# Routing weights spread by DMA instead of by one-hot matmuls, in the second layer of a gated two-layer block

## The chip, the cores and the metric

The kernel runs on one core of one Trainium2 chip. The metric is the device time of one execution in microseconds (us). TensorE (PE in the profile) multiplies matrices, VectorE (DVE), ScalarE (ACT) and GpSimd (POOL) work on elements, SyncE (SP) issues the DMAs. Each engine runs its own instruction list in order, and the engines wait for one another on semaphores. SBUF is the on-chip memory, PSUM the banks that TensorE writes into.

## The reference, cut to what matters

```python
x = L0_attn_data                                     # (4, 512, 512), float32
x = x + s0(norm(x)) * silu(ffn0(norm(x)))            # first layer, untouched here
xn = layernorm(x)
s  = attention(xn)                                   # one head of 128, Wqkv, softmax, Wo
base_out   = xn @ base_w.T + base_b
res_hidden = xn @ A.T                                # 64 values of each row
probs      = softmax(xn @ router_w.T)                # 16 experts
topw, topi = top_k(probs, 2); topw = topw / (sum(topw) + 1e-6)
combine    = sum(one_hot(topi, 16) * topw[..., None], -2)
delta      = einsum('bse,bsr,eor->bso', combine, res_hidden, B)
x = x + s * silu(base_out + 0.5 * delta)
```

The last product, `delta`, is done as one matrix product over 16 x 64 = 1024 rows: row e*64+r is `combine[e] * res_hidden[r]`, and the weights `combine` must therefore be repeated 64 times each over the partitions.

## The kernel before, in words

There are four chunks (one for each of the 4 sequences of 512 rows), and two layers. The second layer takes them in turn, with a first chunk, a loop over two, and a last one. TensorE multiplies float32 numbers as pairs of a rounded part and a rest (`_hi`, `_lo`), three matmuls of 128x128 by 128x512 for a full product (`three`). ScalarE mostly makes the rounded parts, VectorE or GpSimd the rests.

In one chunk of the second layer TensorE does, in this order: `a` (the 64 hidden values and 16 logits), q, k, v; the transposes of the routing weights `comb`; `scores` of four tiles of 128 rows; `base` (the product with `base_w`, 12 matmuls a tile); the transposes of the probabilities (`probs_transpose`, kt 0 to 3); `lora` (the 1024-row product, 24 matmuls a tile); probabilities times v ("PV"); and `project` with Wo. Behind the third tile come the transposes of the next chunk's normalized rows.

Routing: VectorE finds the two largest weights in 19 short steps (`route`). The weights stand in `comb` twice, 32 columns apart. TensorE transposes them, ScalarE copies both copies to `combT`, VectorE replaces the second by the rest (L1129), and `spread` (L1322) multiplies `combT` by a matrix of zeros and ones, `pick`, so that a PSUM bank holds one expert's weight on each of 64 partitions. There are eight such products (kt 0 to 7) in a chunk, one matmul each, in two banks. VectorE's `prods` (L1068) multiplies the bank by `res` into one of three buffers of `prod`, ScalarE rounds it (`prod_hi`, L801), GpSimd makes the rest (`prod_lo`, L672), and `lora` uses both.

The order is written out by hand for each engine. `y`, which gathers `base` and `lora`, alternates between banks 2 and 3, so that the tiles 2 and 3 start `base` late in the chunk. The rows of the next chunk are loaded when the current ones have been transposed and the stores of the chunk before are done; VectorE takes their statistics (L369, L374) behind output tile 0 and 1 and normalizes them (L388), GpSimd makes the reciprocal root (L380, L382) behind its eight rests. GpSimd then multiplies gate and attention and adds the input (`gate`, L394 and L398).

Of the kernel before, what the change touches and what calls it, by code (L numbers as in the profile page):

```python
# [6 lines left out]
P = 128  # L7
BANK = 512

ALU = mybir.AluOpType  # L10
# [8 lines left out]
def block_mask_ffn_then_attention_lora_kernel(  # L19
# [27 lines left out]
    IT = w1.shape[0]  # L47
# [23 lines left out]
    mid_rows = mid.rearrange("b (t p) d -> b p t d", p=P)  # L71

    ctx = ExitStack()
    with ctx:
# [36 lines left out]
        comb = few.take("comb", [P, TT, 2 * Q])  # L111
# [27 lines left out]
        next_c = Span(span_c.start)  # L139
        pick_raw = raw_at("pick_raw", [P, KE, P], next_c.end)  # L140
        pick = next_c.take("pick", [P, KE, P], F32R)

        span_s = Span(phase(max(span_c.end, next_c.end)))
# [30 lines left out]
        prod_hi = next_1h.take("prod_hi", [P, KE, S], F32R)  # L174
        prod_lo = next_1l.take("prod_lo", [P, KE, S], F32R)
        res = next_1h.take("res", [P, S])
        combT = next_1l.take("combT", [P, S], F32R)
# [29 lines left out]
        prod = rest_t.take("prod", [P, 3, S])  # L207
# [88 lines left out]
        pick_ready = sem("pick_ready")  # L296
# [5 lines left out]
        comb_zero = sem("comb_zero")  # L302
        comb_hi = sem("comb_hi")
        comb_split = sem("comb_split")
# [18 lines left out]
        spread_done = sem("spread_done")  # L323
# [116 lines left out]
        y = [banks[2], banks[3]]  # L440
        sc = [banks[4], banks[5]]
        tr = [banks[6], banks[7]]
        NROUTE = 19
# [7 lines left out]
        def _(sp):  # L451
# [75 lines left out]
            def rows_out(c, place, to_next):  # L527

                for tt in range(TT):
                    if to_next:  # L530
                        turn(c + 1, 0, tt)
                    store_row(c, place, tt)
                sp.wait_ge(st_rows, c * TT * 16 + TT * 16)
                sp.sem_inc(g_free, 1)
# [5 lines left out]
            rows_out(0, mid_rows[0], True)  # L540
            with sp.Fori(1, CH - 1) as c:
                chunk(c, x_rows[c + 1], False)
                rows_out(c, mid_rows[c], True)
            chunk(CH - 1, mid_rows[0], True)
            rows_out(CH - 1, mid_rows[CH - 1], False)


            def chunk(c, source):
                g = c + CH
                sp.dma_start(x_res[:], mid_rows[c]).then_inc(ld_res, 16)  # L550
                if source is not None:
                    sp.wait_ge(xT_tr, g * TT + TT)
                    sp.dma_start(x_tile[:], source).then_inc(ld_x, 16)
                for tt in range(TT if source is not None else TT - 1):
                    sp.wait_ge(rows_done, g * TT + tt + 1)
                    sp.dma_start(out_rows[c][:, tt, :], g_tile[:, tt, :]).then_inc(st_out, 16)
                if source is not None:
                    sp.wait_ge(st_out, c * TT * 16 + TT * 16)
                    sp.sem_inc(g_free, 1)
                else:  # L560

                    for i in range(2):
                        sp.wait_ge(end_done, i + 1)
                        sp.dma_start(out_rows[c][:, TT - 1, half(i)], g_tile[:, TT - 1, half(i)]).then_inc(st_out, 16)
                    sp.wait_ge(st_out, CH * TT * 16 + 16)

            with sp.Fori(0, CH - 1) as c:
                chunk(c, mid_rows[c + 1])
            chunk(CH - 1, None)

        @block.gpsimd
        def _(gp):
# [39 lines left out]
            def next_layer():  # L612
# [7 lines left out]
                gp.wait_ge(t_done, CH)  # L620
                gp.memset(pick_raw[:], 0.0).then_inc(pick_ready, 1)
                for q in range(2):
                    gp.wait_ge(pick_ready, q + 1)
                    sq = pick_raw[:].rearrange("e k (h r) -> e k h r", r=R)
                    gp.affine_select(out=sq, in_=sq, compare_op=ALU.not_equal, fill=1.0, base=-q * Q,
                                     pattern=[[-EPT, KE], [-1, EPT], [0, R]], channel_multiplier=1).then_inc(pick_ready, 1)
                gp.wait_ge(pick_ready, 3)
                nc.gpsimd.tensor_copy(pick[:], pick_raw[:]).then_inc(pick_ready, 1)
# [39 lines left out]
            def chunk(c, last):  # L668

                for kt in range(KE):  # L670
                    gp.wait_ge(prod_hi_done, c * KE + kt + 1)
                    nc.gpsimd.tensor_tensor(prod_lo[:, kt, :], prod[:, kt % 3, :], prod_hi[:, kt, :].bitcast(F32),  # L672
                                            ALU.subtract).then_inc(prod_split, 1)
                if not last:
                    rows_rstd(gp, c + CH + 1)
# [8 lines left out]
        def _(act):  # L684
# [114 lines left out]
            def prods_hi(c, kt):  # L799
                act.wait_ge(prod_done, c * KE + kt + 1)  # L800
                nc.scalar.activation(prod_hi[:, kt, :], prod[:, kt % 3, :], ACT.Copy).then_inc(prod_hi_done, 1)  # L801
# [9 lines left out]
            def chunk(c, is_first, last):  # L811
# [8 lines left out]
                for j, src in enumerate((pj[1], sc[0], sc[1])):  # L820
                    if j == 2:
                        act.wait_ge(comb_tr, c + 1)
                        nc.scalar.activation(combT[0:2 * Q, :], tr[0][0:2 * Q, :], ACT.Copy).then_inc(comb_hi, 1)
# [8 lines left out]
                prods_hi(c, 0)  # L832
                prods_hi(c, 1)
                probs_exp(c, 1)
                prods_hi(c, 2)
                prods_hi(c, 3)
                probs_exp(c, 2)
                probs_exp(c, 3)
                prods_hi(c, 4)
                prods_hi(c, 5)  # L840
                probs_hi(c, 0)
                probs_hi(c, 1)
                probs_hi(c, 2)
                probs_hi(c, 3)
                prods_hi(c, 6)
                prods_hi(c, 7)
# [669 lines left out]
```

## Time and profile before

| | before |
|---|---|
| median of 3 runs | 650.63 us (649.14 to 651.12) |
| the profiled execution | 650.05 us, of which the span from the first to the last instruction is 648.2 us |
| TensorE busy | 632.3 us (98%) |
| VectorE, ScalarE, GpSimd busy | 446.3 (69%), 213.4 (33%), 240.0 us (37%) |
| granted TensorE clock | 0.999 of full |
| moved by DMA | 46.16 MB |

A busy share is an average over both layers. What an edit is worth is read where it stands: in the chain of waits, which follows the work that ended last back in time, and in the lists of instructions in order of time, which show what each engine waited for.

### The profile page before, as it was taken

To read this page: it belongs to the slowest core of one execution; us is meant where nothing else is said; L and a number is where in the kernel's file an instruction comes from. 1 tells how busy PE (TensorE), PEld (TensorE's weight loads), DVE (VectorE), ACT (ScalarE), POOL (GpSimd) and SP (SyncE) were. 2 spreads that over 40 slices of the span, in tenths; PEclk is the share of its full clock that TensorE was granted. 3 is DMA by queue.
4 is the path that set the end of the run, shared out by engine and by line. 5 is a ranking of instruction groups with operands and counts; after the bars stand their busy time and mean duration, and the time that the engine had idled before them with its cause. 6 is when DMAs were issued, how large, how long until landed. Compare 5 with 4: busy or idle time off the path is not lost.

```text
span 648.2 us, 8466 instructions
## 1 busy us (share of the span) xinstructions
PE 632.3 (98%) x2942; PEld 509.9 (79%) x2942; DVE 446.3 (69%) x716; ACT 213.4 (33%) x379; POOL 240.0 (37%) x188
## 2 busy tenths in 40 slices
PE   7999999999999999999999999999999999999997
PEld 3768787878888878888878787778878878887887
DVE  7987776787765777765777886655765857575633
ACT  3533333312223312223322243651255035314510
POOL 2355545650000740000742644582425433351441
PEclk9999999999999999999999999999999999999999
DMA  9940000022400022300153622050140013012000
GB/s 282 400 158 1 2 0 1 26 81 52 127 17 9 26 81 70 108 16 8 32 141 95 173 82 73 17 178 1 49 147 1 16 50 129 0 41 89 2 32 33
DMA packets 42575, 46.16 MB, mean 71 GB/s; under 512 B 25072, under 2 KB 25456, under 8 KB 41904
## 3 DMA queue, kind: packets, MB, share of 16 engines
q1 hardware_dynamic: 42544, 45.76, 22.1%
q8 instruction: 18, 0.29, 0.2%
q14 instruction: 13, 0.11, 0.1%
HBM read 31.85 MB, written 8.39 MB: 62 GB/s over the span
## 4 chain that ended last, share of the span: by engine, by line
PE 81%; DVE 12%; issue 3%; ACT 1%; POOL 1%; DMA 1%; DVEq 0%; POOLq 0%; ACTq 0%; SPq 0%
PE bank L418 73%; DVE counts L940 3%; PE bank L348 2%; DVE seg_top L926 2%; DVE eq L928 2%; PE bank L1205 1%; PE bank L1359 1%; DMA first<-counts 1%; PE bank L1183 1%; DVE h_lo L970 1%; PE bank L1322 1%; DVE h L961 1%; POOL g_tile L394 1%; PE bank L1224 1%; DVE ws_raw L994 0%
## 5 line engine op out<-in xcount | busy, mean ns | idle before, releaser
L418 PE MATMUL bank<-w_hi_t,h_hi 128*128 128x512 f32 x224 | 90.4, 404 | 0.7 <-DVE h_lo L970 0.4
L761 ACT ACTIVATE h_hi<-h 128x512 fp32r<-128x512 f32 x56 | 35.4, 633 | 162.9 <-DVE h L961 162.9
L418 PE MATMUL bank<-w_lo_t,h_hi 128*128 128x512 f32 x224 | 87.6, 391 | 0.0
L418 PE MATMUL bank<-xT_hi,w_hi_t 128*128 128x512 f32 x224 | 87.4, 390 | 0.1
L418 PE MATMUL bank<-w_hi_t,h_lo 128*128 128x512 f32 x224 | 87.4, 390 | 0.0
L418 PE MATMUL bank<-xT_hi,w_lo_t 128*128 128x512 f32 x224 | 87.2, 389 | 0.0
L418 PE MATMUL bank<-xT_lo,w_hi_t 128*128 128x512 f32 x224 | 87.1, 389 | 0.0
L940 DVE TENSOR_TENSOR_SCAN counts<-restart,eq 128x512 bf16<-128x512 bf16 (+1 forms) x56 | 76.0, 1357 | 2.4
L394 POOL TENSOR_TENSOR g_tile<-g_tile,s_tile 128x512 f32<-128x512 f32 x31 | 44.3, 1430 | 88.3 <-DVE g_tile L983 44.2
L926 DVE TENSOR_REDUCE seg_top<-bank 128x16 f32<-128x512 f32 (+1 forms) x64 | 39.5, 617 | 46.2 <-PE bank L1205 46.2
L672 POOL TENSOR_TENSOR prod_lo<-prod,prod_hi 128x512 fp32r<-128x512 f32 x32 | 40.6, 1291 | 57.9 <-ACT prod_hi L801 57.8
L970 DVE TENSOR_TENSOR h_lo<-h,h_hi 128x512 fp32r<-128x512 f32 x56 | 42.0, 751 | 27.0 <-ACT h_hi L761 25.4
L380 POOL TENSOR_TENSOR rstd<-mean_var,eps 128x4 f32<-128x4 f32 x8 | 1.6, 201 | 159.1 <-DVE mean_var L374 159.1
L740 ACT ACTIVATE h<-bank 128x512 f32<-128x512 f32 x56 | 33.5, 598 | 57.4 <-DVE h_lo L970 47.3
L418 PE MATMUL bank<-b_hi,prod_hi 128*128 128x512 f32 (+1 forms) x136 | 52.1, 383 | 0.0
L418 PE MATMUL bank<-b_hi,prod_lo 128*128 128x512 f32 (+1 forms) x136 | 51.3, 377 | 0.0
L418 PE MATMUL bank<-b_lo,prod_hi 128*128 128x512 f32 (+1 forms) x136 | 51.3, 377 | 0.0
L418 PEld LDWEIGHTS bank<-w_hi_t,h_hi 128*128 128x128 f32 x224 | 42.1, 188 | 10.7 <-DVE h_lo L970 2.3
L418 PEld LDWEIGHTS bank<-w_hi_t,h_lo 128*128 128x128 f32 x224 | 42.1, 188 | 9.4
L418 PEld LDWEIGHTS bank<-xT_hi,w_hi_t 128*128 128x128 f32 x224 | 42.0, 188 | 9.1 <-ACT s_tile L695 0.4
L418 PEld LDWEIGHTS bank<-xT_hi,w_lo_t 128*128 128x128 f32 x224 | 42.0, 188 | 8.7
L418 PEld LDWEIGHTS bank<-xT_lo,w_hi_t 128*128 128x128 f32 x224 | 42.1, 188 | 8.7
(191 smaller groups left out, 1300.5 us busy)
## 6 DMA issues: line engine op xcount, KB each, us to landing
w_raw<-in_w SPq DMA_DIRECT2D x28, 256.0 KB, 10.1
x_res<-in_x SPq DMA_DIRECT2D x4, 1024.0 KB, 8.5
mid_state<-g_tile SPq DMA_DIRECT2D x16, 256.0 KB, 2.1
x_tile<-mid_state SPq DMA_DIRECT2D x4, 1024.0 KB, 7.4
x_res<-mid_state SPq DMA_DIRECT2D x4, 1024.0 KB, 5.5
out<-g_tile SPq DMA_DIRECT2D x15, 256.0 KB, 2.0
x_tile<-in_x SPq DMA_DIRECT2D x3, 1024.0 KB, 5.6
b_raw<-in_lora_b SPq DMA_DIRECT2D x2, 1024.0 KB, 5.1
```

Of the source, the lines that this page charges most:

```text
L348: last = nc.tensor.transpose(rows_bank(g, tt)[:, k * P:(k + 1) * P], x_tile[:, tt, k * P:(k + 1) * P], ident[:])
L394: nc.gpsimd.tensor_tensor(g_tile[:, tt, :], g_tile[:, tt, :], s_tile[:, tt, :], ALU.mult).then_inc(s_free, 1)
L418: last = nc.tensor.matmul(dst, a, b, start=(start and n == 0), stop=(stop and n == len(mms) - 1))
L672: nc.gpsimd.tensor_tensor(prod_lo[:, kt, :], prod[:, kt % 3, :], prod_hi[:, kt, :].bitcast(F32), ALU.subtract).then_inc(prod_split, 1)
L740: nc.scalar.activation(h[:], up[it % 2][:], ACT.Relu).then_inc(relu_done, 1)
L761: nc.scalar.activation(h_hi[:, it % 2, :], h[:], ACT.Copy).then_inc(h_hi_done, 1)
L926: nc.vector.reduce_max(seg_top[:, 0:segs], got, AX.X).then_inc(seg_max, 1)
L928: nc.vector.tensor_tensor(eq[:, 0:PW[p]].rearrange("p (s n) -> p s n", n=SEG), got, seg_top[:, 0:segs, None].to_broadcast([P, segs, SEG]), ...
L940: nc.vector.tensor_tensor_scan(kept[:, tt, 0:PW[p]], restart[:, 0:PW[p]], eq[:, 0:PW[p]], 0.0, ALU.mult, ALU.add).then_inc(sel_count, 1)
L961: nc.vector.scalar_tensor_tensor(h[:], which, 1.0, h[:], ALU.is_equal, ALU.mult).then_inc(h_masked, 1)
L970: nc.vector.tensor_tensor(h_lo[:, it % 2, :], h[:], h_hi[:, it % 2, :].bitcast(F32), ALU.subtract).then_inc(h_split, 1)
L1183: last = nc.tensor.matmul(sel[:], c1_stack[:, k, :], x[:, k, :], start=(k == 0 and x is xT_hi), stop=(k == KD - 1 and x is xT_lo))
```

## The change

It has these parts, all in the second layer:

- the weights stand in `comb` once, and one step of `route` goes; ScalarE copies the 16 transposed rows to `combT`, the rest of them is not made, and `pick` and `spread` go;
- SyncE stores `combT` (16 rows of 2 KB) to DRAM, waits for it, and reads it back with eight DMAs into `prod`, each on 64 partitions with every row repeated 64 times, 256 KB each, 2 MB in all;
- `prods` multiplies `prod` in place in eight buffers of its own, both inputs in SBUF;
- each tile's `y` has its own bank (0 to 3), so that `base` of the tiles 1, 2 and 3 moves ahead of the probabilities and PV, and `lora` of a tile is no longer interleaved with another's;
- the next rows are loaded before the stores of output tiles 2 and 3, their statistics are taken amid the score maxima, and they are normalized ahead of the products;
- SyncE issues the weights' DMAs of the next chunk behind the last store of the current one.

```diff
-        y = [banks[2], banks[3]]
+        y = [banks[tt] for tt in range(TT)]
...
+            def weights_out(c):
+
+                sp.wait_ge(comb_out, c + 1)
+                sp.dma_start(weights, combT[0:E, :]).then_inc(st_weights, 16)
+                sp.wait_ge(st_weights, c * 16 + 16)
+                for i in range(4):
+                    for j in range(EPT):
+                        sp.dma_start(prod[j * R:(j + 1) * R, i * KG:(i + 1) * KG, :],
+                                     weights_of[j:j + 1, i * KG:(i + 1) * KG, :].to_broadcast([R, KG, S])).then_inc(ld_spread[i], 16)
...
             def chunk(c, source):
...
                 sp.dma_start(x_res[:], mid_rows[c]).then_inc(ld_res, 16)
+                out_row(c, 0)
+                out_row(c, 1)
                 if source is not None:
...
+                    rows_after(c + 1, source)
+                out_row(c, 2)
+                out_row(c, 3)
+                sp.wait_ge(st_out, c * TT * 16 + TT * 16)
+                sp.sem_inc(g_free, 1)
+                weights_out(c + 1)
...
             def chunk(c, last):
 
+                if not last:
+                    rows_rstd(gp, c + CH + 1)
                 for kt in range(KE):
                     gp.wait_ge(prod_hi_done, c * KE + kt + 1)
-                    nc.gpsimd.tensor_tensor(prod_lo[:, kt, :], prod[:, kt % 3, :], prod_hi[:, kt, :].bitcast(F32),
+                    nc.gpsimd.tensor_tensor(prod_lo[:, kt, :], prod[:, kt, :], prod_hi[:, kt, :].bitcast(F32),
                                             ALU.subtract).then_inc(prod_split, 1)
-                if not last:
-                    rows_rstd(gp, c + CH + 1)
...
             def prods(c, kt):
 
-                dve.wait_ge(spread_done, c * KE + kt + 1)
-                if kt >= 3:
-                    dve.wait_ge(prod_split, c * KE + kt - 2)
-                nc.vector.tensor_tensor(prod[:, kt % 3, :], pj[kt % 2][:], res[:], ALU.mult).then_inc(prod_done, 1)
+                dve.wait_ge(ld_spread[kt // KG], c * EPT * 16 + EPT * 16)
+                nc.vector.tensor_tensor(prod[:, kt, :], prod[:, kt, :], res[:], ALU.mult).then_inc(prod_done, 1)
...
-                pe.wait_ge(comb_split, c + 1)
-                spread(c, 0)
-                spread(c, 1)
                 scores(c, 1)
                 base(c, 0, 1, KD)
-                spread(c, 2)
-                spread(c, 3)
                 scores(c, 2)
+                base(c, 1, 0, 2)
                 scores(c, 3)
-                base(c, 1)
-                spread(c, 4)
-                spread(c, 5)
+                base(c, 1, 2, KD)
+                base(c, 2)
                 probs_transpose(c, 0)
                 probs_transpose(c, 1)
+                if not last_chunk:
+                    base(c, 3, 0, 2)
+                probs_transpose(c, 2)
+                probs_transpose(c, 3)
+                if not last_chunk:
+                    base(c, 3, 2, KD)
                 if is_first:
                     pe.wait_ge(b_split, KE)
                 lora(c, 0, 0, 4)
-                probs_transpose(c, 2)
-                probs_transpose(c, 3)
-                spread(c, 6)
-                spread(c, 7)
-                lora(c, 1, 0, 4)
                 pe.wait_ge(p_split, c * TT + TT)
```

VectorE, the first chunk, from the first score maximum (`s_max`) to the last product (`prod`), before:

```order
L1059 TENSOR_REDUCE s_max<-bank 128x1 [waits score_done]
L1061 TENSOR_SCALAR s_neg<-s_max 128x1 [waits score_max]
L1068 TENSOR_TENSOR prod<-bank,res 128x512 [waits spread_done] x2
L1134 TENSOR_TENSOR v_lo<-bank,v_hi 128x512 [waits v_hi_done]
...
L1068 TENSOR_TENSOR prod<-bank,res 128x512 [waits prod_split,spread_done] x2
L1072 TENSOR_TENSOR pT_lo<-bank,pT_hi 128x512 [waits p_hi_done] x4
L1068 TENSOR_TENSOR prod<-bank,res 128x512 [waits prod_split,spread_done] x2
```

and the same place now, from the third score maximum on:

```order
L1069 TENSOR_REDUCE s_max<-bank 128x1 [waits score_done]
L1071 TENSOR_SCALAR s_neg<-s_max 128x1 [waits score_max]
L385 TENSOR_SCALAR x_tile<-x_tile,mean_var,rstd 128x512 [waits rstd_step]
L385 TENSOR_SCALAR x_tile<-x_tile,mean_var,rstd 128x512 x3
L1076 TENSOR_TENSOR prod<-prod,res 128x512 [waits ld_spread_0] x2
L1076 TENSOR_TENSOR prod<-prod,res 128x512 [waits ld_spread_1] x2
L1080 TENSOR_TENSOR pT_lo<-bank,pT_hi 128x512 [waits p_hi_done] x2
L1076 TENSOR_TENSOR prod<-prod,res 128x512 [waits ld_spread_2] x2
L1080 TENSOR_TENSOR pT_lo<-bank,pT_hi 128x512 [waits p_hi_done] x2
L1076 TENSOR_TENSOR prod<-prod,res 128x512 [waits ld_spread_3] x2
```

All eight products now stand behind the last score maximum and the normalization, and none waits for GpSimd any more; they wait for DMAs (`ld_spread`).

ScalarE in the same place, before (`prod_hi` and `pT_hi` are the rounded products and probabilities) and now:

```order
L801 ACTIVATE prod_hi<-prod 128x512 [waits prod_done] x2
L805 ACTIVATE pT_hi<-bank 128x512 [waits p_tr] x4
L801 ACTIVATE prod_hi<-prod 128x512 [waits prod_done] x2
```

```order
L818 ACTIVATE prod_hi<-prod 128x512 [waits prod_done] x3
L822 ACTIVATE pT_hi<-bank 128x512 [waits p_tr] x2
L818 ACTIVATE prod_hi<-prod 128x512 [waits prod_done]
L822 ACTIVATE pT_hi<-bank 128x512 [waits p_tr] x2
L818 ACTIVATE prod_hi<-prod 128x512 [waits prod_done] x4
```

Three rounded products now stand ahead of the first rounded probabilities, and four behind the last.

## Rows read from the trace of the kernel before

**Rows 1.** The page: TensorE's busy time, share and instructions.

```profile
PE 632.3 (98%) x2942; PEld 509.9 (79%) x2942; DVE 446.3 (69%) x716; ACT 213.4 (33%) x379; POOL 240.0 (37%) x188
```

**Rows 2.** Chain of waits, second layer: start us, us, engine, line, count.

```profile
480.28 2.09 PE bank L418 x9
482.37 0.44 PE bank L1413 x4
482.81 0.47 PE bank L1322 x2
...
491.01 0.88 PE bank L1359 x8
...
495.96 23.81 PE bank L418 x105
...
539.22 2.09 PE bank L418 x9
```

**Rows 3.** What TensorE waited for, 395 to 648.2 us: total, times, longest.

```profile
PE bank L1359 <- ACT probs L796: 1.4, 1, 1.4
```

**Rows 4.** VectorE in order of time: start, us, instruction, count, idle before.

```profile
488.30 0.69 DVE L1059 TENSOR_REDUCE s_max<-bank 128x1 f32<-128x512 f32 x1
489.03 0.15 DVE L1061 TENSOR_SCALAR s_neg<-s_max 128x1 f32<-128x1 f32 x1
...
495.72 1.29 DVE L1072 TENSOR_TENSOR pT_lo<-bank,pT_hi 128x512 fp32r<-128x512 f32 x2 [1.14 <-ACT pT_hi L805]
...
512.60 5.81 DVE L388 TENSOR_SCALAR x_tile<-x_tile,mean_var,rstd 128x512 f32<-128x512 f32 x4 [1.41 <-POOL rstd L382]
```

**Rows 5.** VectorE, the same normalization in the first layer.

```profile
399.51 1.91 DVE L388 TENSOR_SCALAR x_tile<-x_tile,mean_var,rstd 128x512 f32<-128x512 f32 x4
```

**Rows 6.** ScalarE in order of time, the same chunk.

```profile
480.32 0.59 ACT L823 ACTIVATE combT<-bank 64x512 fp32r<-64x512 f32 x1 [1.12 <-PE bank L1401]
...
489.88 0.19 ACT L796 ACTIVATION_READ_ACCUMULATOR probs<-bank,s_neg 128x1 f32 x1
491.54 1.23 ACT L801 ACTIVATE prod_hi<-prod 128x512 fp32r<-128x512 f32 x2 [1.47 <-DVE prod L1068]
492.68 1.07 ACT L805 ACTIVATE pT_hi<-bank 128x512 fp32r<-128x512 f32 x2
```

**Rows 7.** GpSimd in order of time, chunks 0 and 1.

```profile
426.08 1.29 POOL L398 TENSOR_TENSOR g_tile<-g_tile,x_res 128x512 f32<-128x512 f32 x1
427.34 7.60 POOL L672 TENSOR_TENSOR prod_lo<-prod,prod_hi 128x512 fp32r<-128x512 f32 x6
...
471.66 1.28 POOL L398 TENSOR_TENSOR g_tile<-g_tile,x_res 128x512 f32<-128x512 f32 x1
...
511.55 1.02 POOL L382 TENSOR_TENSOR rstd<-rstd,neg_half 128x4 f32<-128x4 f32 x1
```

**Rows 8.** GpSimd, first layer's end, both inputs in SBUF.

```profile
391.29 1.29 POOL L643 TENSOR_TENSOR b_lo<-b_raw,b_hi 128x512 fp32r<-128x512 f32 x1
392.54 1.72 POOL L643 TENSOR_TENSOR b_lo<-b_raw,b_hi 128x512 fp32r<-128x512 f32 x1
```

**Rows 9.** VectorE beside them, both inputs in SBUF.

```profile
393.10 1.71 DVE L961 SCALAR_TENSOR_TENSOR h<-first,h 128x512 f32<-128x512 bf16 x1
395.51 1.00 DVE L970 TENSOR_TENSOR h_lo<-h,h_hi 128x512 fp32r<-128x512 f32 x1 [0.70 <-ACT h_hi L761]
398.90 0.69 DVE L970 TENSOR_TENSOR h_lo<-h,h_hi 128x512 fp32r<-128x512 f32 x1 [0.70 <-ACT h_hi L761]
```

**Rows 10.** DMA issues: size in KB, median us from issue to landing; then one issue on SyncE.

```profile
out<-g_tile SPq DMA_DIRECT2D x15, 256.0 KB, 2.0
bias_a<-in_bo SPq DMA_DIRECT2D x1, 256.0 KB, 8.5
476.15 0.41 SPq L550 DMA_DIRECT2D x_res<-mid_state  x1
```

**Rows 11.** Stretches: us, busy us of each engine, clock, DMA share, GB/s.

```profile
354.00:356.00 2.00, 2.00 (x11) 1.65 (x10) 1.42 (x2) 0.55 (x1) 2.00 (x2) 1.00 1.00 356
```

## What the change should do to the time

> **What bounds the kernel now.** I read the page first. TensorE is busy 98% of the span [rows 1], so time goes only where its instructions go, or where the change makes it wait. The chain of waits, read over the second layer, says the same more sharply: from the middle of the first chunk on it is TensorE's own instructions without a gap, one chunk every 539.22 - 480.28 = 58.94 us, and a matmul in a long run costs 23.81 / 105 = 0.227 us [rows 2]. The list of TensorE's waits has one entry of size there, 1.4 us in the first chunk for the exponentials of the scores [rows 3]. Behind it stands GpSimd, which works on the first layer's gates until 427.4 and only then makes product rests [rows 7]; VectorE had three product buffers, stood still for them, and took its score maxima late. Last come the lists in order of time of VectorE, ScalarE and GpSimd [rows 4 to 9], for what may become late.
>
> **What goes.** `spread` is two matmuls in 0.45 to 0.47 us [rows 2], so 8 in a chunk are 1.85 us and 32 are 7.4 us, all in the chain. The 1.4 us of the first chunk goes too, since VectorE no longer waits for a product buffer ahead of its maxima. Together 8.8 us, if nothing else waits. The rest of `combT`, one routing step and `pick` lie on VectorE and GpSimd off the chain: nothing.
>
> **The transfer.** ScalarE's copy of `combT` ends at 480.32 + 0.59 = 480.9 [rows 6]. A store of 256 KB lands 2.0 us after issue, and an issue takes 0.41 us of SyncE [rows 10]. For the 32 KB store I take the 2.0: the weights are in DRAM at 483.0. The eight reads are issued in 8 x 0.41 = 3.3 us; at the 356 GB/s of a stretch full of loads [rows 11] 2.1 MB take 5.9 us, so the first pair lands at about 483.0 + 0.8 + 2.0 = 485.8 and the last at 483.0 + 2.0 + 5.9 = 491. The bias was a load that repeats one row over the partitions; it landed in 8.5 us behind 2 MB of others [rows 10], which those 2 MB alone explain. So repeated rows seem to cost nothing extra. The first product is wanted at 491.1 (below), the seventh at about 500: hidden, with 5 us in hand. The store is not late by SyncE either: the gate of the last tile ended at 471.66 + 1.28 [rows 7], its store lands 2 us later, at 475, and SyncE waits for the weights from then on. The input rows for the residual are issued behind the reads, and are wanted only when the gates start. The next rows arrive long before their statistics. All nothing.
>
> **The products, the term that decides.** Before, TensorE had `lora` of tile 0 and 1 spread over the chunk and the products came in pairs. Now all eight come behind the last score maximum. I go through chunk 1 with the clock of the trace, everything up to 480.28 being as it was. TensorE: 9 matmuls, the v transposes (2.09 + 0.44, [rows 2]), then 24 matmuls to the end of the fourth scores, 5.44: 488.25. Another 18 for `base`: 492.33; two groups of probability transposes (0.88): 493.21; 6 of `base`: 494.57. There it wants the third group, which needs the rests of the first two groups.
>
> VectorE: the last maximum starts at 488.3 as before and ends with `s_neg` at 489.2 [rows 4]. The normalization took 5.81 us for four in the middle of GpSimd's gates [rows 4], and 1.91 us where GpSimd was idle [rows 5]; it is idle now: 491.1. Products follow each other by 0.60 (1.29 for two less the overlap, as in the pair of [rows 4]). So product 0, 1, 2 end at 491.8, 492.4, 493.0, and ScalarE, 0.63 each, gives the first rounded product at 492.5.
>
> From here VectorE and GpSimd both want two inputs from SBUF, which `prods` did not before (one input was a bank). What that costs stands at the end of the first layer. GpSimd's subtraction takes 1.29 us alone and 1.72 beside such a VectorE instruction [rows 8]; the VectorE instruction issued at 393.10 ended at 394.81, 0.55 after GpSimd's at 392.54 + 1.72 = 394.26, and took 1.71, another 1.00, against 0.69 alone [rows 9]. So they alternate: a product costs GpSimd 0.43, and ends 0.55 after GpSimd's instruction. The Trainium skill says it more harshly (SBUF — State Buffer, "Who interferes with whom"): whoever issues first holds the shared pair for the whole instruction and the other fully blocks. By that a product costs GpSimd 0.6 and not 0.43; the trace shows 0.43.
>
> GpSimd's rest 0 then ends at 494.2, product 3 at 494.7, the two probability rests at 495.3 and 495.9. TensorE waits 0.8 for the first and 0.15 for the second: 496.45; 6 more of `base`: 497.8. Rest 1 ends at 495.8, rest 2 at 497.1, rest 3 at 498.75; `lora` takes a pair of rounded product and rest every 0.68 and is through the first four at 500.5. Products 4 and 5 end at 497.6 and 499.3, the probability rests 2 and 3 at 499.9 and 500.5: PV waits 0.1 and ends at 503.3. Rests 4 to 7 end at 500.0, 501.7, 503.9 and 505.2, where TensorE wants the last at 505.4. It ends the piece at 506.05; without a wait it would be 493.21 + 48 x 0.227 + 0.88 = 504.98. New waits: 1.1 us. Behind this point TensorE has 24 matmuls a tile and VectorE some 2 us of work a tile, so the tail stays TensorE's. Chunks 1 and 2: -1.85 + 1.1 = -0.75 each.
>
> Chunk 0: the gates end at 427.4, and the reciprocal root behind them, some 1.3 us (its longer part is 1.02, [rows 7]), at 428.7, where VectorE would want it at 489.2 less the 60.7 between the chunks, 428.5: 0.3 with the handover. -1.85 - 1.4 + 1.1 + 0.3 = -1.85.
>
> Chunk 3 has no next rows, so its products start 1.9 us earlier, but it has no `base` of tile 3 to lay between the transposes, 12 matmuls or 2.7 us of cover. The same steps give the third group at 494.2 (wanted at 493.21, 1.0 late), the fourth 0.15, a rest 0.4 and the probability rests 1.1: 2.6 in all. -1.85 + 2.6 = +0.75.
>
> Sum: -1.85 - 2 x 0.75 + 0.75 = -2.6 us on the profiled 650.05, so 647.4. The median of the runs is 0.6 above it; I forecast for the median 650.63 - 2.6 = 648.0, rounded to 647.9.
>
> What the trace doesn't show is how the two engines behave when both have a row of such instructions queued. Its bounds: a product delays GpSimd by nothing (1.29 alone, the other end of [rows 8]) or by its whole 0.6. At nothing and with no blocking of VectorE, product 3 ends at 493.6, the waits shrink to 0.6, and to 1.0 in chunk 3. I take 0.43 since two rows have it.
>
> **The rivals.** (1) No contention that matters: -8.8 + 3 x 0.6 + 1.0 + 0.3 = -5.7, 644.9. For it: the normalization beside the gates left GpSimd's instructions near 1.35. Against: [rows 8].
>
> (2) Slower: GpSimd's rests become the chain. If each of the five products queued behind GpSimd's start goes first and costs it 0.6 plus a handover, the eight rests need 8 x 1.26 + 5 x 0.7 = 13.6 from 493.1 and the last ends at 506.7, 1.3 behind its time; with the blocked probability rests ahead TensorE waits 2.45 a chunk, and 3.9 in the last. -8.8 + 3 x 2.45 + 3.9 + 0.3 = +2.75, 653.4. It decides from 1.85 us of waits a chunk on. The skill's rule above, taken literally, leads here.
>
> (3) The transfer comes late. It decides from a first pair landed after 491.1, 10.2 us behind the copy of `combT`, and costs every later microsecond in each of four chunks. If the repeated rows came at a quarter of the rate, the last pair would land at 509, 9 late: 650.6 + 36 - 9 = about 678. [Rows 10] speak against it.
>
> (4) Everything is covered, no waits at all: -8.8, 641.8. Against it stands that ScalarE's first two probability roundings are behind three products.
>
> **How the numbers follow.** A measurement of this kernel tells 0.3% from no change, 1.95 us: faster is below 648.7. Chances: the forecast 0.48 (own range 646 to 650), (1) 0.22, (2) 0.18, (3) 0.05, (4) 0.07. Faster: two thirds of the first, all of (1) and (4): 0.60. Within 0.3%: the rest of the first and a third of (2), 0.22. Slower 0.18. The range, 643.0 to 653.0, leaves out (3) and (4) and the tails.
>
> **What would show it.** Right: no matmuls on `combT`, 0 us for `probs` in the first chunk, a chunk period of about 58.2, TensorE waits for `pT_lo` of 0.5 to 1 us ahead of the third group, products of 1.0 to 1.8 us where GpSimd is busy, normalization in 1.9. Wrong: a wait of VectorE on a DMA ahead of the products (rival 3), TensorE's long waits on `prod_lo` (rival 2), products of 0.69 throughout (rival 1).

## The result and the profile after

The changed kernel takes 646.61 us (median of 9 runs, 645.60 to 649.72) and the kernel before, beside it on the same chip, 650.63 (9 runs, 649.14 to 651.64). The ratio is 0.9944 [0.993, 0.9958], so 3.6 us less, between 2.7 and 4.6; the two medians lie 4.0 us apart. The forecast was 647.9 with a range of 643.0 to 653.0. The profiled execution took 645.60 us with a span of 643.8; before it was 650.05 with 648.2.

The page after; its TensorE line answers to [rows 1]. Columns: busy us, share of the span, instructions.

```profile
PE 627.2 (97%) x2910; PEld 503.0 (78%) x2910; DVE 442.9 (69%) x706; ACT 213.5 (33%) x379; POOL 245.1 (38%) x184
```

The 32 matmuls of `spread` are gone. They were 7.4 us of the chain, and the span fell by 4.4. The wait of 1.4 us for `probs` and 1.5 us of the first layer went as well, so some 6 us came back as waiting and what it leaves behind. Where, the list of TensorE's waits after says, from 395 us to the end: total us, times, longest. It answers to [rows 3].

```profile
PE bank L1364 <- DVE pT_lo L1080: 1.6, 4, 1.0
PE bank L415 <- POOL prod_lo L691: 0.7, 3, 0.2
PE bank L345 <- DVE x_tile L385: 0.5, 1, 0.5
PE bank L415 <- DVE pT_lo L1080: 0.4, 1, 0.4
```

The wait for `probs` is gone, and waits for the rests of the probabilities and of the products are new. TensorE in order of time after, start and us: the transposes of the routing weights at the head of chunks 1 and 2, the third group of probability transposes and the last `lora` step of chunk 1, and two places in the last chunk. What stands in brackets is the idle time ahead. It counts from the modelled end of the matmul before, 0.39 us behind its start; without a wait the next one starts at 0.227 us already, so the time lost at a wait is some 0.16 us more than the number in brackets.

```profile
476.06 0.60 PE L1406 MATMUL bank<-ident,comb 128*16 128x128 f32 x4
...
491.21 1.25 PE L1364 MATMUL bank<-ident,probs 128*128 128x128 f32 x8 [0.20 <-DVE pT_lo L1080]
...
501.74 0.50 PE L415 MATMUL bank<-b_hi,prod_hi 128*128 128x512 f32 x1 [0.21 <-POOL prod_lo L691]
...
534.48 0.60 PE L1406 MATMUL bank<-ident,comb 128*16 128x128 f32 x4
...
607.43 1.25 PE L1364 MATMUL bank<-ident,probs 128*128 128x128 f32 x8 [0.98 <-DVE pT_lo L1080]
...
611.79 0.50 PE L415 MATMUL bank<-pT_hi,v_hi 128*128 128x512 f32 x1 [0.37 <-DVE pT_lo L1080]
```

A chunk now takes 534.48 - 476.06 = 58.42 us instead of 58.94. I cut both kernels' second layer at these transposes, whose starts before were 419.16, 479.69, 538.62 and 597.56, and after 417.64, 476.06, 534.48 and 592.88:

| piece | before | after | difference | forecast |
|---|---|---|---|---|
| chunk 0 | 60.53 | 58.42 | -2.11 | -1.85 |
| chunk 1 | 58.93 | 58.42 | -0.51 | -0.75 |
| chunk 2 | 58.94 | 58.40 | -0.54 | -0.75 |
| chunk 3, to the end | 50.68 | 50.92 | +0.24 | +0.75 |
| second layer (with 0.05 ahead of it) | | | -2.97 | -2.6 |
| first layer | | | -1.47 | 0 |

The second layer did what was forecast, to 0.4 us. The first layer gave 1.5 us that nobody had asked for.

The piece of chunk 1 on which the forecast rested, VectorE after (start, us, instruction, idle before), answering to [rows 4]. All times here are 479.69 - 476.06 = 3.63 us earlier than on the prediction's clock.

```profile
485.44 0.15 DVE L1071 TENSOR_SCALAR s_neg<-s_max 128x1 f32<-128x1 f32 x1
485.55 1.92 DVE L385 TENSOR_SCALAR x_tile<-x_tile,mean_var,rstd 128x512 f32<-128x512 f32 x4
487.38 2.50 DVE L1076 TENSOR_TENSOR prod<-prod,res 128x512 f32<-128x512 f32 x4
490.46 1.29 DVE L1080 TENSOR_TENSOR pT_lo<-bank,pT_hi 128x512 fp32r<-128x512 f32 x2 [0.58 <-ACT pT_hi L822]
...
492.74 1.78 DVE L1076 TENSOR_TENSOR prod<-prod,res 128x512 f32<-128x512 f32 x1
```

GpSimd after, its first rest of the chunk alone, then all eight as one group:

```profile
488.81 2.22 POOL L691 TENSOR_TENSOR prod_lo<-prod,prod_hi 128x512 fp32r<-128x512 f32 x1 [5.28 <-ACT prod_hi L818]
...
488.81 12.87 POOL L691 TENSOR_TENSOR prod_lo<-prod,prod_hi 128x512 fp32r<-128x512 f32 x8 [5.28 <-ACT prod_hi L818]
```

Normalization and four products follow `s_neg` without a pause. The first rest begins at 488.81, while VectorE is in its third product and has the fourth queued; both run through, the fourth ends at 489.9, and the rest takes 2.22 us. From then on a product beside a rest takes up to 1.78, and a rest beside a product 1.74 to 1.84. Two of these rests alone, and the four products of the last chunk, where the first rest did come in ahead of the fourth:

```profile
492.23 1.74 POOL L691 TENSOR_TENSOR prod_lo<-prod,prod_hi 128x512 fp32r<-128x512 f32 x1
...
495.65 1.84 POOL L691 TENSOR_TENSOR prod_lo<-prod,prod_hi 128x512 fp32r<-128x512 f32 x1
...
602.33 3.59 DVE L1076 TENSOR_TENSOR prod<-prod,res 128x512 f32<-128x512 f32 x4
```

The transfer, from the page's DMA issues of the changed kernel (KB each, median us from issue to landing) and SyncE's issue of the eight reads:

```profile
prod<-expert_weights SPq DMA_DIRECT2D x32, 256.0 KB, 5.4
expert_weights<-combT SPq DMA_DIRECT2D x4, 32.0 KB, 1.6
...
478.90 5.15 SPq L552 DMA_DIRECT2D prod<-expert_weights  x8
```

No wait of VectorE on a DMA stands ahead of the products in this kernel: the transfer is hidden.

### The profile page after: what moved, and what is told of

It is laid out like the page before. It is cut to its first block, busy times and chain, and to the rows that moved or that the text cites. A ratio compares the mean times of both kernels' runs of the same rounds, so it can differ in the third digit from the quotient of the medians.

```text
span 643.8 us, 8382 instructions
## 1 busy us (share of the span) xinstructions
PE 627.2 (97%) x2910; PEld 503.0 (78%) x2910; DVE 442.9 (69%) x706; ACT 213.5 (33%) x379; POOL 245.1 (38%) x184
## 4 chain that ended last, share of the span: by engine, by line
PE 61%; issue 16%; DVE 12%; POOL 9%; ACT 1%; DMA 1%; POOLq 0%; DVEq 0%; ACTq 0%; SPq 0%
PE bank L415 56%; POOL prod_lo L691 4%; DVE counts L952 3%; POOL g_tile L391 2%; DVE seg_top L938 2%; POOL g_tile L395 2%; DVE eq L940 2%; PE bank L345 1%; PE bank L1213 1%; DMA first<-counts 1%; PE bank L1191 1%; DVE h_lo L982 1%; DVE h L973 1%; POOL rstd L379 1%; PE bank L1232 1%
## 5 line engine op out<-in xcount | busy, mean ns | idle before, releaser
L391 POOL TENSOR_TENSOR g_tile<-g_tile,s_tile 128x512 f32<-128x512 f32 x31 | 45.7, 1473 | 107.2 <-DVE g_tile L1102 56.5
L952 DVE TENSOR_TENSOR_SCAN counts<-restart,eq 128x512 bf16<-128x512 bf16 (+1 forms) x56 | 74.3, 1327 | 2.4
L691 POOL TENSOR_TENSOR prod_lo<-prod,prod_hi 128x512 fp32r<-128x512 f32 x32 | 51.2, 1634 | 31.5 <-ACT prod_hi L818 31.5
```

The source lines that it names most:

```text
L391: nc.gpsimd.tensor_tensor(g_tile[:, tt, :], g_tile[:, tt, :], s_tile[:, tt, :], ALU.mult).then_inc(s_free, 1)
L691: nc.gpsimd.tensor_tensor(prod_lo[:, kt, :], prod[:, kt, :], prod_hi[:, kt, :].bitcast(F32), ALU.subtract).then_inc(prod_split, 1)
L952: nc.vector.tensor_tensor_scan(kept[:, tt, 0:PW[p]], restart[:, 0:PW[p]], eq[:, 0:PW[p]], 0.0, ALU.mult, ALU.add).then_inc(sel_count, 1)
```

## The experiments

Each is an edit of the changed kernel unless it is said otherwise, and is compared with the kernel before on the same chip. "Period" is the time between two heads of chunks as above.

**again** and **pick_back** ask whether the 1.47 us of the first layer repeat, and where they come from. Edit of pick_back:

```diff
+                gp.memset(pick_raw[:], 0.0).then_inc(pick_ready, 1)
+                for q in range(2):
...
+                    gp.affine_select(out=sq, in_=sq, compare_op=ALU.not_equal, fill=1.0, base=-q * Q,
...
+                nc.gpsimd.tensor_copy(pick[:], pick_raw[:]).then_inc(pick_ready, 1)
                 gp.wait_ge(ld_bo, 16)
```

> The changed kernel once more, beside the variants below, so that they are compared on one chip. Theory A (the second layer gave 3.0 us of the 4.4 us between the two profiles, the first layer 1.5 us, of which 0.8 us is chance in how GpSimd and VectorE take turns around 224 to 237 us): about 646.5 us, with a place around 224 to 237 us that differs from profile to profile by up to 0.9 us in either kernel. Rival B (that 0.8 us belongs to the change): it comes back the same in every profile of the changed kernel.

> The changed kernel with GpSimd making the matrix of zeros and ones in the first layer again (a memset, two selections, a cast, 4.7 us of GpSimd around 360 us), which nothing reads. Theory A: those instructions held VectorE off SBUF and TensorE waited for it, so the run is 0.5 to 0.7 us slower than the changed kernel, all of it between 359 and 369 us, and VectorE's h_lo there takes 1.5 us again and not 0.69. Rival B: the 0.66 us between the profiles at that place is chance, and the run is equal to the changed kernel within 0.2 us.

again: 645.85 us, ratio 0.9944 [0.9931, 0.9958]. pick_back: 646.59, 0.995 [0.9937, 0.9964], and span 644.5 against 643.7. Before, two groups of matmuls in the first layer stood 362.48 to 368.82, 6.34 us apart; after, 361.67 to 367.34, 5.67; in pick_back 361.61 to 367.95, again 6.34. The rows of VectorE and GpSimd there, pick_back:

```profile
360.62 2.73 POOL L656 TENSOR_SCALAR_AFFINE_SELECT pick_raw<-pick_raw 128x1024 f32<-128x1024 f32 x2 [0.15 <-POOL pick_raw L652]
360.83 1.50 DVE L996 TENSOR_TENSOR h_lo<-h,h_hi 128x512 fp32r<-128x512 f32 x1 [0.70 <-ACT h_hi L792]
363.68 1.85 DVE L966 TENSOR_TENSOR_SCAN counts<-restart,eq 128x512 bf16<-128x512 bf16 x1
```

and the changed kernel without `pick`:

```profile
360.88 0.69 DVE L982 TENSOR_TENSOR h_lo<-h,h_hi 128x512 fp32r<-128x512 f32 x1 [0.70 <-ACT h_hi L778]
363.55 1.22 DVE L952 TENSOR_TENSOR_SCAN counts<-restart,eq 128x512 bf16<-128x512 bf16 x1
```

GpSimd's building of `pick` held the rest of `h` for 0.8 us and the scan for 0.6, and TensorE waited on that. That is 0.66 us of the 1.47, shown by taking it out and putting it back. The other 0.85 us lie at 224 to 237 us, far from any edit. In the profiles of all kernels here that place has one of two lengths; short in eight, after, again and pick_back among them, and long in six, before and norm_late among them. The kernels both and both_2 below are one kernel, and it was short in one and long in the other; before_no_spread, whose first layer is that of before, had it short. So these 0.85 us are chance and not the change. Why there are two lengths was not settled. There is a second such place, at 13 to 23 us: against the changed kernel it is longer by 1.5 us in the profile of norm_late, 1.1 in that of both and 1.9 in that of both_2, while the others agree there to 0.5 us. So in what follows the period and the last piece tell what an edit did; between medians 1 us can be chance.

**norm_late** asks what the normalization amid the maxima costs. It moves it behind the silu of output tile 0.

```diff
-                if not last:
-                    rows_norm(dve, c + CH + 1)
...
+                    if tt == 0 and not last:
+                        rows_norm(dve, c + CH + 1)
```

> The changed kernel with the normalization of the next rows behind output tile 0 and not ahead of the products; the load, the statistics and the root stay early. Theory A (the 1.3 us a chunk that TensorE loses between the probability transposes and the end of the first lora come from the product chain starting late): the products start when ScalarE has done the last exponential, some 1 to 1.9 us earlier, TensorE's waits there go nearly to zero in the chunks 0 to 2, and the run is 2 to 3.5 us faster than the changed kernel, 643 to 644.5 us. Rival B (GpSimd's chain with VectorE's insertions sets the end whatever the start): under 1 us faster. Rival C: the normalization beside GpSimd's gates takes 3 to 5.8 us, output tile 1 comes late, and the run is slower.

641.82 us, ratio 0.9874 [0.9859, 0.9889], the best so far. (The profiled execution is the longest of its four, 644.02 us, by the two places of chance in the first layer.) VectorE, norm_late:

```profile
486.54 3.60 DVE L1076 TENSOR_TENSOR prod<-prod,res 128x512 f32<-128x512 f32 x4
...
504.59 3.86 DVE L385 TENSOR_SCALAR x_tile<-x_tile,mean_var,rstd 128x512 f32<-128x512 f32 x4
```

TensorE's waits on `pT_lo`, same kernel, second layer:

```profile
PE bank L1364 <- DVE pT_lo L1080: 1.0, 1, 1.0
```

The products start 486.54 - 477.06 = 9.5 us behind the head of the chunk instead of 487.38 - 476.06 = 11.3. The period is 57.12 = 58.94 - 1.82: no new wait is left in chunks 0 to 2, and the one on the list is the last chunk's. The normalization takes 3.86 us instead of 1.92 at its new place, among the gates, and nobody waits for it. So none of the 1.3 us of new waits per chunk is left once its 1.9 us are gone from the old place.

**last_cover** asks whether three quarters of `base` of tile 2, laid between the transposes in the last chunk, take its waits away.

```diff
-                base(c, 2)
+                base(c, 2, 0, 1 if last_chunk else KD)
                 probs_transpose(c, 0)
                 probs_transpose(c, 1)
+                if last_chunk:
+                    base(c, 2, 1, KD)
```

> The changed kernel with three quarters of the base product of tile 2 in the last chunk moved between the second and the third group of probability transposes, so that TensorE has 9 matmuls (2.0 us) to do while it waits for the rests of the first two groups. The transposes start 2.0 us earlier. Theory A: the 0.98 us wait of the last chunk goes and the 0.37 us ahead of probabilities times v stays or grows to 0.6: 0.8 to 1.2 us faster than the changed kernel. Rival B: the rests of the products are what ends last, and the time turns up ahead of the last lora steps: under 0.3 us.

645.92 us, 0.9939 [0.9925, 0.9952]; the last piece takes 50.84 us against 50.92: nothing. The waits, last_cover:

```profile
PE bank L415 <- POOL prod_lo L691: 1.3, 4, 0.7
...
PE bank L1364 <- DVE pT_lo L1080: 0.6, 3, 0.2
```

The wait of 1.0 for `pT_lo` went, and 0.7 for a product's rest came behind it. Behind the first wait GpSimd's rests are nearly as late.

**bank_factor** asks what the two engines cost each other: the products take one factor from a bank, as `spread`'s did.

```diff
+                if kt == 0:
+                    dve.wait_ge(exp_done, c * TT + TT)
-                nc.vector.tensor_tensor(prod[:, kt, :], prod[:, kt, :], res[:], ALU.mult)
+                nc.vector.tensor_tensor(prod[:, kt, :], prod[:, kt, :], sc[1][:], ALU.mult)
```

> The changed kernel with the products taken with a PSUM bank (the one of the third score tile, idle then) in place of res as the second factor, so that they have one input in SBUF; the output is not the reference's. Everything else, DMAs too, is as in the changed kernel; the first product of a chunk also waits for the last exponential. Theory A (products and GpSimd's rests take turns at SBUF): no product above 0.75 us, the eight rests of a chunk take 10.1 to 10.6 us in place of 12.9, the 0.38 us wait ahead of the last lora step goes, and the run is 1 to 3 us faster than the changed kernel. Rival B (the stretched instructions have another cause, the DMA writes into SBUF at the same time for one): products of 1 to 1.8 us remain and the rests still take 12.9.

642.81 us, 0.989 [0.9875, 0.9905]; period 57.7, last piece 50.29. VectorE and GpSimd, bank_factor:

```profile
487.73 2.47 DVE L1078 TENSOR_TENSOR prod<-prod,bank 128x512 f32<-128x512 f32 x4
...
489.15 10.05 POOL L691 TENSOR_TENSOR prod_lo<-prod,prod_hi 128x512 fp32r<-128x512 f32 x8 [5.27 <-ACT prod_hi L818]
...
492.00 1.27 DVE L1078 TENSOR_TENSOR prod<-prod,bank 128x512 f32<-128x512 f32 x2
```

This kernel leaves out the multiplication by `res`. A rest takes 10.05 / 8 = 1.26 us instead of 12.87 / 8 = 1.61, and products follow each other by 0.6 us throughout. The transfers are as before, so they are not what stretches the instructions. The contention is worth 0.7 us a chunk. About 0.6 of the 1.3 us of waits remain without it, with the normalization at the old place. The two parts are not separate: without the 1.9 us of normalization ahead of the products (norm_late) no wait of either part is left, though the contention is still there.

**store_four**, **store_two** and **late_store_two** measure the transfer's room by storing the weights four or two times in series; the third is norm_late with two stores.

```diff
-                sp.dma_start(weights, combT[0:E, :]).then_inc(st_weights, 16)
-                sp.wait_ge(st_weights, c * 16 + 16)
+                for n in range(4):
+                    sp.dma_start(weights, combT[0:E, :]).then_inc(st_weights, 16)
+                    sp.wait_ge(st_weights, c * 64 + 16 * n + 16)
```

> The changed kernel with the store of the weights done four times, each waited for, before they are read back: the reads start 3 x about 1.6 to 1.9 = 5 to 6 us later. In the changed kernel the first pair lands at 483.6 us and is wanted at 487.4 us, the last at 490.4 for 495.6. Theory A (the transfer is hidden with 3.8 us to spare, and costs its lateness one for one beyond that): the first pair is 1 to 2 us late in chunks 0 to 2 and 3 to 4 us late in the last, so VectorE waits for DMA there and the run is 4 to 10 us slower than the changed kernel. Rival B (slack behind the products soaks it up): under 2 us slower. Rival C (the transfer was already late): slower by 4 x 5.5 = 22 us.

> The changed kernel with the store of the weights done twice in series, so that everything read back comes about 1.9 us later. Theory A (3.8 us to spare for the first pair): the second store is hidden whole, the chunk period stays at 58.4 us, and the run is equal to the changed kernel within 0.3 us. Rival B (the transfer already costs something): 1 us or more slower.

> The same second store in the kernel with the late normalization, where the first product is wanted 9.5 us behind the transposes of the weights and the first pair, now 1.9 us later, lands 9.4 us behind them. Theory A: just hidden or late by a few tenths; the period goes from 57.1 us to at most 57.6, the run is 0 to 1.5 us slower than with one store. Rival B: slower by 1.9 us a chunk, 7 us.

store_two: 646.91 us, 0.9954 [0.994, 0.9967], periods 58.42, 58.42 and 58.40, unchanged. The reads start 1.6 us later and land 1.9 us later, and in the chunks 0 to 2 that is hidden. In the last chunk it is not. There the products start 1.9 us earlier, and VectorE waited for the second pair:

```profile
605.24 2.93 DVE L1077 TENSOR_TENSOR prod<-prod,res 128x512 f32<-128x512 f32 x2 [0.80 <-DMA prod<-expert_weights]
```

The last piece took 51.4 us instead of 50.9. The rest of the 1 us above again is the place at 224 to 237, long in this profile.

late_store_two: 644.77, 0.9923 [0.991, 0.9937], period 57.8, which is 0.7 more than norm_late: with earlier products the room is smaller, and two stores end it. Here 0.7 us of lateness cost 0.7 us. VectorE, late_store_two:

```profile
486.98 3.10 DVE L1077 TENSOR_TENSOR prod<-prod,res 128x512 f32<-128x512 f32 x2 [0.68 <-DMA prod<-expert_weights]
```

store_four: 663.12 us, 1.0205 [1.0183, 1.0227]. That is 17 us more than again: above the 4 to 10 of theory A and below the 22 of rival C, which store_two rules out besides. TensorE and VectorE in order of time, store_four:

```profile
493.16 1.29 DVE L1077 TENSOR_TENSOR prod<-prod,res 128x512 f32<-128x512 f32 x2 [1.02 <-DMA prod<-expert_weights]
495.11 3.00 DVE L1077 TENSOR_TENSOR prod<-prod,res 128x512 f32<-128x512 f32 x2 [0.66 <-DMA prod<-expert_weights]
498.76 1.76 PE L1365 MATMUL bank<-ident,probs 128*128 128x128 f32 x7 [3.09 <-DVE pT_lo L1081]
```

and stretches of it: us, busy us of TensorE, its weight load, VectorE, ScalarE and GpSimd, granted clock, DMA share, GB/s.

```profile
496.00:499.00 3.00, 0.23 (x1) 0.24 (x2) 3.00 (x4) 2.23 (x4) 3.00 (x2) 0.80 1.05 264
499.00:502.00 3.00, 3.00 (x12) 2.71 (x12) 3.00 (x4) 1.83 (x4) 1.51 (x3) 0.50 0.67 256
502.00:505.00 3.00, 3.00 (x10) 2.35 (x9) 3.00 (x4) 1.03 (x2) 3.00 (x3) 0.56 0.00 0
505.00:510.00 5.00, 5.00 (x24) 4.12 (x23) 1.64 (x3) 1.14 (x2) 2.89 (x2) 1.00 0.00 0
```

VectorE waited 1.7 us for data. The products then stood ahead of the probability rests and met GpSimd's queue, and TensorE stood still for 3.09 us. Its granted clock fell to 0.50, the 1.2 GHz level, before TensorE went on, and did not come back before some 504.6: the row from 502 has 0.56 in the mean, which is 0.50 for 2.6 us and then 1.00. In between a matmul took 0.43 us instead of 0.227. With periods of 62.07, 63.23 and 62.40, data 1.7 us late cost 3.7 to 4.8 us a chunk. Part of that is the clock. An estimate from these rows: TensorE worked from 498.76 to 504.6 at the lower clock, and 5.8 x (1 - 0.227 / 0.43) is 2.7 of the 4.8 us of this chunk. The other 2.1 are about what the data were late.

**before_no_spread** is an edit of the kernel before: the 32 `spread` matmuls are left out and nothing else is moved.

```diff
-                dve.wait_ge(spread_done, c * KE + kt + 1)
+                dve.wait_ge(proj_read, c * 4 + 4)
-                spread(c, 0)
-                spread(c, 1)
...
```

> The kernel before without its 32 spread matmuls; the products read what the projections left in the banks, and the output is not the reference's. No DMA, no new order. Theory A (a spread matmul costs TensorE its 0.23 us and nothing else): 7.4 us faster than before, 643.2 us, with the 1.4 us wait of the first chunk still there. It says what the freed matmuls would be worth where nothing new waits, and so what the new order and the transfer cost. Rival B: the products come no earlier, other waits fill the place, and it is under 5 us faster.

646.73 us, 0.9963 [0.9946, 0.998]; periods 60.39, 57.94 and 57.95. The kernel leaves out the spreading of the weights, and its products read what stands in the banks. Only 1.0 us a chunk came of the 1.85. TensorE's waits, before_no_spread:

```profile
PE bank L1359 <- ACT probs L796: 2.4, 1, 2.4
...
PE bank L418 <- ACT probs L796: 0.4, 2, 0.2
```

With less on TensorE the first chunk waits 2.4 us for `probs`, where it was 1.4 [rows 3], and the scores wait in the chunks 1 and 2: the products of the old order stand ahead of the maxima on VectorE. Taking the matmuls out is not enough alone. That placing the products behind the maxima is what frees the rest fits both kernels, but no run moves the products and nothing else.

**both**, **both_2** and **norm_late_2** ask whether last_cover adds to norm_late, and take the best version again. The edits are the two above together. The last chunk has no next rows to normalize, so norm_late moves nothing there.

> Late normalization and the moved base product together. Theory A: the two gains add, 3 to 4.5 us faster than the changed kernel, 642 to 643.5 us. Rival B: they overlap or are small, under 1.5 us.

> The kernel with the late normalization once more, beside the next one, on one chip. Theory A: 641.5 to 643 us, a chunk period of 57.1 us; the place around 224 to 237 us may fall either way by 0.9 us.

> Late normalization and the moved base product once more. Theory A (the moved product only shifts the last chunk's wait from the probability rests to the product rests, as it did alone): equal to the late normalization alone within 0.5 us. Rival B: 0.8 us or more faster, as it was first expected.

both: 642.71 us, 0.9887 [0.9871, 0.9903]; both_2: 642.83, 0.9888 [0.9873, 0.9903]; norm_late_2: 643.08, 0.99 [0.9884, 0.9915]. The last piece takes 50.8 us in both, 51.2 in both_2 and 50.9 in norm_late. They are the same within the intervals: the gain of 0.8 us and more for last_cover is refuted. The best version is the changed kernel with the late normalization: 641.8 and 643.1 us when taken twice, 1.0 to 1.3% below the kernel before and some 0.6% below the changed kernel.

## Why the prediction was right, step by step

The forecast held: faster, 1.3 us from the median, by the mechanism it named. Of the 4.45 us between the two profiled executions, the second layer gave 2.97 against 2.6. That its waits came so near the forecast is in part luck: those ahead of the transposes were half of what was forecast, and waits for the last rests, forecast at nothing, made up for them.

- **What goes.** 1.85 us a chunk and the 1.4 of the first were there in full. norm_late shows it: without new waits the period is shorter by 1.82.
- **The new waits.** In chunk 1 they are 1.85 - 0.52 = 1.3 us; the forecast had 1.1. On its clock less 3.63 TensorE wanted the third group at 490.94 and came at 490.85; there `pT_lo` held it for 0.36 (forecast 0.8), the fourth group for 0.22 (0.15), the fourth `lora` step for 0.1 (0), and the last one, at 501.74, for 0.38 (0); the 0.1 forecast for PV did not come. These are 1.06. A wait also leaves something behind: the matmul after the last one is followed at 0.33 us and not 0.227, 0.1 more, a term that I did not have. The last 0.1 us lies in steps of a few hundredths each. The step that was mis-sized is the turn of the two engines. I let GpSimd in behind the third product, so that the fourth ended at 491.07; VectorE ran all four without a stop and ended at 489.88, and GpSimd's first rest ended at 491.03 instead of 490.57. So the probabilities came earlier than I had them. The last rest ended at 488.81 + 12.87 = 501.68, forecast 501.57, so the price of the contention was right in sum; TensorE, less held up before, now met it.
- **Rival 1** (no contention) is what bank_factor shows: its price was 58.94 - 1.85 + 0.6 = 57.69 a chunk, and the period was 57.7. In the changed kernel it did not hold, by 0.7 us a chunk. **Rival 2** (the rests as the chain) had the last rest at 506.7 - 3.63 = 503.1 and it ended at 501.7; the waits stayed below the 1.85 from which it decides. The eight rests together are 12.87 - 10.05 = 2.8 us over those of bank_factor. Of these the first rest has 0.93 (2.22 against the 1.29 of [rows 8]), for one product under way and one queued, and the four beside the last four products have 0.45 to 0.55 each (1.74 to 1.84), close to the 0.43 that I took. A product held by a rest ended 0.55 us behind the rest's end, as in the prediction: the one of 492.74 at 494.52, the rest of 492.23 at 493.97. The Trainium skill (SBUF — State Buffer, "Who interferes with whom") has the one issued later fully blocked. The trace agrees with that for the held products: none ended before the rest beside it. It does not agree on which one is held: the fourth product starts in the profile at 489.2, behind the first rest's 488.81, and ran ahead of it. Nor does it bear out the whole 0.6 us a product that the prediction worked out from this rule. **Rival 4** (no waits) was false here and is true of the chunks 0 to 2 of norm_late.
- **The transfer.** Hidden, as forecast, but not by its numbers. The eight issues took 5.15 us and not 3.3, the reads ran at about 245 GB/s and not 356, and the store landed in 1.6 us and not 2.0. Single issues with their landing times put the first pair at 483.7, wanted at 487.4, and the last at 490.3, wanted at 495.7. The room of the first pair was 3.7 us where the forecast had 5. The second pair had less, and the forecast did not look at it: it landed at 485.9 and was wanted at 488.6, so 2.7 us. In the last chunk it landed at 602.8 and was wanted at 603.5, so 0.7 us, which is why store_two cost time there alone. **Rival 3**'s price of one for one held in late_store_two (0.7 us late, 0.7 a chunk). In store_four it did not: more than two for one, by the estimate above about half of it through the clock.
- **Chunk 0 and the last chunk.** -2.11 for -1.85, and +0.24 for +0.75. In the last chunk the waits are 1.0, 0.2 and 0.4, with what they leave behind 2.1, not 2.6. The turn of the engines was the forecast one there (3.59 us for four products), and so were the first two waits. The waits that were sized too large are 0.4 for a rest of a product, which did not come, and 1.1 for the last probability rests, which was 0.4.
- **"The rest lies off the chain: nothing."** This failed for `pick`, which I priced by its own engine. It was worth 0.66 us (pick_back) through VectorE's slower instructions beside it. The other 0.85 us of the first layer are chance. Without the 1.47 us of the first layer the profiled execution would have come within 0.4 us of the forecast.

## What to carry to other kernels

When an instruction is put ahead of a queue on an engine, count it against the first thing behind it that the bounding engine wants: 1.9 us of normalization at a place where VectorE looked free cost 1.3 us a chunk, and behind the silu, taking twice as long, it cost none. Work of an engine that waits for nobody is still not free if its neighbour shares its access to SBUF. And measure the room of a hidden transfer by making it late, and for each piece of it: here the second pair had the least, 2.7 us in the middle chunks and 0.7 in the last. Once that was used up, 0.7 us of lateness cost 0.7 us, and 1.7 us, with TensorE's clock falling in the wait, 3.7 to 4.8.

## What the runs showed of the hardware

- **Turns.** Where a GpSimd instruction with inputs from SBUF came up beside a row of VectorE's with two, the turns differed. In chunk 1 of the changed kernel VectorE's fourth product went first as well, and the GpSimd instruction waited (2.22 us against 1.29 alone in [rows 8]). In its last chunk and in norm_late the GpSimd instruction went ahead of the fourth product (four products in 3.59 and 3.60 us, not 2.50), though it came up 0.2 to 0.3 us into the third product each time. Behind that they alternated, and both paid: the VectorE instruction 1.78 against 0.69, the GpSimd instruction 1.74 to 1.84 against 1.29. What decides the first turn is not settled.
- **Other instructions of GpSimd hold VectorE too.** In pick_back its affine select stood beside a VectorE subtraction of 1.50 us, and the cast that ends `pick`'s building beside a scan of 1.85; they took 0.69 and 1.22 without it.
- **Repeated rows.** Reads from DRAM that repeat one row over 64 partitions ran at 245 GB/s and took 0.64 us of SyncE each; the plain load behind them ran at 369 and took 0.41. They differ also in the partitions, 64 against 128, so the repeating alone is not shown to be the cause. Stretches of the changed kernel, columns as above:

```profile
484.00:486.00 2.00, 2.00 (x10) 1.65 (x10) 1.26 (x3) 0.74 (x3) 0.00 (x0) 1.00 1.06 245
...
490.00:492.00 2.00, 1.80 (x11) 1.11 (x10) 1.54 (x3) 1.53 (x4) 2.00 (x2) 1.00 0.95 369
```

- **The clock.** Waits of 0.2 to 1.0 us left the granted clock at 1.00, and so did the 2.4 us in before_no_spread; in the one of 3.09 us in store_four it fell to 0.50.
